# Second attention: the product of values and turned probabilities as one float32 product instead of three float32r products

## The reference

```python
x = x + ffn(cond(x))       # cond: adaptive layer norm, attention of 16 heads, feed-forward
# ffn, first half: the second attention, 16 query heads, 4 key/value heads, width 128
h = rmsnorm(hidden, attn_norm_w)
q, k, v = h @ q_w.T, h @ k_w.T, h @ v_w.T
q, k = apply_rope(rmsnorm(q, q_norm_w)), apply_rope(rmsnorm(k, k_norm_w))
attn = einsum('bhqk,bhkd->bhqd', softmax(mask(q k^T * scale)), repeat(v, 4))
hidden = hidden + attn @ o_w.T
# ffn, second half: 8 experts, the best 2 for each token, weighted
```

## Time and profile before

| | us |
|---|---|
| Median of 3 runs | 1257.84 (1256.36 to 1258.54) |
| The profiled execution | 1245.22 |
| Its span, first to last instruction | 1243.5 |
| PE busy in the span | 1154.7 (93%), 7776 matmuls |
| DVE busy | 793.6 (64%) |
| ACT busy | 655.5 (53%) |
| POOL busy | 520.4 (42%) |
| Mean granted PE clock | 0.984 of full speed |

### The profile page before, as it was taken

One profiled execution on the slowest core, in us unless ns is written; L12 is line 12 of the kernel. 1 busy time (PEld: TensorE's weight loads), 2 busy tenths in 40 slices (PEclk: granted clock), 3 DMA queues, 4 the chain that ended last, 5 costly groups with the idle time before them and its releaser, 6 DMA issues.

```text
span 1243.5 us, 23075 instructions
## 1 busy us (share of the span) xinstructions
PE 1154.7 (93%) x7776; PEld 1040.7 (84%) x7808; DVE 793.6 (64%) x1699; ACT 655.5 (53%) x1866; POOL 520.4 (42%) x597
## 2 busy tenths in 40 slices
PE   6999999999999999989988999998999999758995
PEld 5888999999999999978876888987887898657895
DVE  3666554345434553367557888888787888757666
ACT  3445444444444444465545766656756665545553
POOL 4111131113111311143347656665875786633753
PEclk9999999999999999999999999999999999989998
DMA  9100000000000011041001029400000100223546
GB/s 339 59 1 1 18 1 18 1 1 1 18 1 1 1 38 48 1 186 35 18 18 52 1 78 302 125 2 1 23 14 1 56 23 5 47 71 106 172 130 199
DMA packets 46454, 68.81 MB, mean 55 GB/s; under 512 B 4741, under 2 KB 38537, under 8 KB 45355
## 3 DMA queue, kind: packets, MB, share of 16 engines
q1 hardware_dynamic: 42595, 58.89, 15.2%
q0 software_dynamic: 3744, 8.43, 1.9%
HBM read 41.17 MB, written 27.97 MB: 56 GB/s over the span
## 4 chain that ended last, share of the span: by engine, by line
PE 67%; DVE 9%; ACT 6%; issue 4%; POOL 3%; DMA 2%; SPq 0%; ACTq 0%; DVEq 0%; POOLq 0%
PE bank L1770 12%; PE bank L1807 9%; PE bank L1958 7%; PE bank L1838 6%; PE bank L2015 5%; PE bank L1798 4%; PE bank L1780 4%; PE bank L2148 4%; PE bank L2107 3%; PE bank L2179 2%; ACT p L891 2%; PE bank L2042 2%; PE bank L1899 2%; PE bank L1788 2%; PE bank L2074 1%
## 5 line engine op out<-in xcount | busy, mean ns | idle before, releaser
L570 POOL TENSOR_TENSOR p<-p,rinv 128x512 f32<-128x512 f32 x64 | 66.5, 1040 | 409.3 <-DVE rinv L1340 409.3
L891 ACT ACTIVATE p<-bank,nb,rq 128x128 f32<-128x128 f32 x256 | 113.9, 454 | 133.4 <-DVE nb L1556 133.3
L760 ACT ACTIVATE p<-bank,nmax 128x128 f32<-128x128 f32 x256 | 90.7, 367 | 117.1 <-DVE nmax L1328 117.1
L644 POOL TENSOR_TENSOR qr<-qr,rb 128x512 f32<-128x512 f32 x64 | 81.6, 1276 | 95.7 <-DVE rb L1514 95.1
L1336 DVE COPY pt<-bank 128x512 f32<-128x512 f32 x64 | 44.2, 691 | 107.2 <-PE bank L1788 104.4
L1770 PE MATMUL bank<-cur_hi,wqk_hi 128*128 128x512 f32 x256 | 108.6, 424 | 4.1 <-DVE cur_lo L1281 4.1
L1770 PE MATMUL bank<-cur_hi,wqk_lo 128*128 128x512 f32 x256 | 101.5, 397 | 0.0
L1770 PE MATMUL bank<-cur_lo,wqk_hi 128*128 128x512 f32 x256 | 101.4, 396 | 0.0
L769 ACT ACTIVATE o_hi<-bank,bqkv 128x512 fp32r<-128x512 f32 x64 | 44.2, 691 | 100.3 <-PE bank L1798 100.0
L1344 DVE SCALAR_TENSOR_TENSOR o_lo<-bank,bqkv,o_hi 128x512 fp32r<-128x512 f32 x64 | 48.0, 751 | 52.8 <-ACT o_hi L769 52.8
L2107 PE MATMUL bank<-k_t,q_t 128*128 128x128 f32 x512 | 68.3, 277 | 12.3 <-ACT p L891 10.5
(11 more groups left out here) (271 smaller groups left out, 3880.5 us busy)
## 6 DMA issues: line engine op xcount, KB each, us to landing
token_scratch<-empty SPq DMA_DIRECT2D x1, 13287.0 KB, 47.3
xs<-token_scratch SPq DMA_DIRECT2D x46, 129.0 KB, 2.2
wqk_raw<-in_wqk SPq DMA_DIRECT2D x8, 512.0 KB, 10.6
gate<-gates_scratch SPq DMA_DIRECT2D x8, 512.0 KB, 3.9
got_t<-expert_scratch SPq DMA_DIRECT2D x16, 256.0 KB, 3.7
w_raw<-in_w SPq DMA_DIRECT2D x2, 1408.0 KB, 6.3
xres<-in_x SPq DMA_DIRECT2D x4, 512.0 KB, 9.5
wv_raw<-in_wv SPq DMA_DIRECT2D x8, 256.0 KB, 10.5
```

What stands on the lines that cost most here:

```text
L570: nc.gpsimd.tensor_tensor(p1[:, h % 2], p1[:, h % 2], rinv[:, h % 2].unsqueeze(2).broadcast_to([P, GB, T]), ALU.mult).then_inc(a_pn, 1)
L644: nc.gpsimd.tensor_tensor(qr[:, s.u % 2], qr[:, s.u % 2], rb[:], ALU.add).then_inc(g_qr, 1)
L760: last = nc.scalar.activation(p1[:, h % 2, b], bank[3][:, b * T:(b + 1) * T], ACT.Exp, bias=nmax[:, h % 2, b:b + 1], accum_out=rsum[:, h % ...
L891: last = nc.scalar.activation(p2[:, (s.u - 3) % 2, j], bank[3][:, j * T:(j + 1) * T], ACT.Exp, scale=rq[:, (s.u - 3) % 4, j:j + 1], bias=n ...
```

## The change

Values and turned probabilities are kept as one float32 tile each. ACT still makes the two copies (L924, L931), now of type float32. The two subtractions on DVE go. PE makes one float32 product of 512 columns in place of three float32r products, and every wait that stood on `g_pl` or `g_vl` stands on the copies' own semaphores, `g_ph` and `g_vh`.

```diff
-        v_hi = sb("v_hi", [P, 2, HKV * DH], F32R, at=W2 + 24 * KB)
-        v_lo = sb("v_lo", [P, 2, HKV * DH], F32R, at=W2 + 28 * KB)
+        v2 = sb("v2", [P, 2, HKV * DH], at=W2 + 24 * KB)
-        pt_hi = sb("pt_hi", [P, REP * T], F32R, at=W2 + 36 * KB)
-        pt_lo = sb("pt_lo", [P, REP * T], F32R, at=W2 + 38 * KB)
+        pt2 = sb("pt2", [P, REP * T], at=W2 + 36 * KB)
...
-                    nc.scalar.activation(pt_hi[:], bank[5][:], ACT.Copy).then_inc(g_ph, 1)
+                    nc.scalar.activation(pt2[:], bank[5][:], ACT.Copy).then_inc(g_ph, 1)
...
-                    nc.scalar.activation(v_hi[:, s.b % 2], bank[2][:], ACT.Copy).then_inc(g_vh, 1)
+                    nc.scalar.activation(v2[:, s.b % 2], bank[2][:], ACT.Copy).then_inc(g_vh, 1)
...
-                if s.live(4):
-                    dve.wait_ge(g_ph, n - 3)
-                    nc.vector.tensor_tensor(pt_lo[:], bank[5][:], pt_hi[:].bitcast(F32), ALU.subtract).then_inc(g_pl, 1)
-                if new_seq:
-                    dve.wait_ge(g_vh, s.seq + 1)
-                    nc.vector.tensor_tensor(v_lo[:, s.b % 2], bank[2][:], v_hi[:, s.b % 2].bitcast(F32),
-                                            ALU.subtract).then_inc(g_vl, 1)
...
-                    pe.wait_ge(g_pl, n - 4)
-                    pe.wait_ge(g_vl, s.g * GB + (s.u - 5) // HKV + 1)
+                    pe.wait_ge(g_ph, n - 4)
+                    pe.wait_ge(g_vh, s.g * GB + (s.u - 5) // HKV + 1)
...
-                    for i, (l, r) in enumerate(split_products(v_hi[:, slot, ks], v_lo[:, slot, ks], pt_hi[:], pt_lo[:])):
-                        last = pe.matmul(bank[6][:], l, r, start=(i == 0), stop=(i == 2))
-                    last.then_inc(g_pvp, 1)
+                    pe.matmul(bank[6][:], v2[:, slot, ks], pt2[:], start=True, stop=True).then_inc(g_pvp, 1)
...
-                        pe.wait_ge(g_pl, n - 4)
+                        pe.wait_ge(g_ph, n - 4)
...
-                    pe.wait_ge(g_vl, s.g * GB + 3)
+                    pe.wait_ge(g_vh, s.g * GB + 3)
...
-                    pe.wait_ge(g_pl, NG * 4 * GB)
+                    pe.wait_ge(g_ph, NG * 4 * GB)
```

More of the change, by code:

```diff
@@ L293, in program @@
             sem(f"g_{x}") for x in ("ex", "ksq", "sq", "ph", "vh", "qt", "oh", "kt"))
-        g_x, g_mx, g_nb, g_kb, g_qb, g_ks, g_kr, g_pl, g_ss, g_ri, g_vl, g_ol = (
-            sem(f"g_{x}") for x in ("x", "mx", "nb", "kb", "qb", "ks", "kr", "pl", "ss", "ri", "vl", "ol"))
+        g_x, g_mx, g_nb, g_kb, g_qb, g_ks, g_kr, g_ss, g_ri, g_ol = (
+            sem(f"g_{x}") for x in ("x", "mx", "nb", "kb", "qb", "ks", "kr", "ss", "ri", "ol"))
         g_ka, g_rk, g_kv, g_qr, g_rq, g_qv, g_pn = (
@@ L2022, in values @@
                     if s.had(4):
-                        pe.wait_ge(g_vl, s.seq)
+                        pe.wait_ge(g_vh, s.seq)
                     if s.u == 12 and not s.first:
@@ L2114, in step @@
                 if s.u == 15 and not s.first:
-                    pe.wait_ge(g_vl, GB * (s.g + 1))
+                    pe.wait_ge(g_vh, GB * (s.g + 1))
                     ranks(s.g - 1, bank[2])
```

## The result

| | before, us | after, us | ratio, 95% interval |
|---|---|---|---|
| First comparison, medians | 1257.87 | 1246.74 | 0.9922 (0.9903 to 0.9941) |
| Second | 1253.65 | 1245.15 | 0.9933 (0.9911 to 0.9955) |
| Third | 1245.99 | 1237.81 | 0.9925 (0.9898 to 0.9952) |
| Profiled execution, first comparison | 1245.22 | 1249.14 | |

The change makes the kernel faster by 0.7 to 0.8% of its time: 11.1, 8.5 and 8.2 us. I had forecast 5.5. The two first profiles alone say the opposite, 4 us slower, and the reason lies in stages whose instructions the change leaves alone.

The account below looks back on a forecast made before the run. PE's own work was taken to bound most of the second attention, DVE and ACT its end. +9.5 - 7.0 - 4.0 - 4.2 + 0.2 = -5.5 us, from 1257.8 to 1252.3 us, range 1248.5 to 1261.

Parts of the forecast that it names:

- PE's price up to the last PE-bound steps: Weighted values before 1056 us: one float32 product costs PE 0.17 us more per step, 56 steps, +9.5 us.
- Relief in groups two to four: Steps 13 to 15 and step 1 behind them: earlier row maxima take back 7.0 of PE's 7.6 us of waits.
- Relief in the first group: From 670 to 750 us: 4.0 of PE's 6.3 us of waits come back, bounds 2 and 6.
- The end, 58th to last row maximum: From 1056 to 1089 us, chain over DVE and ACT: 1.6 + 2.6 = 4.2 us less.
- Behind it, to the first expert tile: The last weighted values lie on the chain behind the end part: +0.2 us.
- the rival of a costlier pass: A pass with 128 stationary columns costs over 0.43 us: +0.22 to 0.23 per step, about 1255.5 us; chance 0.17.
- What stays behind `pt_lo`: On DVE, routing and the row maximum stand behind `pt_lo`; in a routing step they move up by 0.87 us.
- The lead out of the new-sequence steps: Without both subtractions DVE's row maximum comes earlier in the step with a new sequence ahead: lead of 1.3 to 1.8 us.
- The three steps of 0.87: In the end part, three steps with `pt_lo` on the chain give 0.87 us each, 2.6 us.
- The waits stay: Rival: the row maximum comes no earlier in routing steps, only PE's price is left, 1268 to 1271 us; chance 0.13.
- The end is held by something else: Rival: POOL or the transfers are late, the end's 4.2 us shrink to 0 to 2, about 1255 us; chance 0.12.
- More comes free: Rival: all 7.6 and 6.3 us of waits recovered, the end gains 5: -9, so 1249 us; chance 0.10.

Follow-up runs that it names:

- dve_only: Kernel after, but PE makes three float32r products of the high parts, low parts left out, both subtractions gone: 1235.80 us, ratio 0.9861 to the kernel before.
- pe_only: Kernel before with one float32 product on PE, both DVE subtractions and PE's waits for them kept: 1261.12 us against 1253.65, ratio 1.0052.
- pt_gone: Kernel before without the `pt_lo` subtraction, its product replaced by a repeated one, `v_lo` kept: 1235.21 us against 1246.03, ratio 0.9919.

## Why the forecast was wrong, by its steps

The mechanism was right, and so was each sign but that of the smallest term; the size was too small, and the measured time fell 2 us below my range. A part of that is the scatter of the first comparison: the 9.1 us that the stages show, off my 1257.8, would be 1248.7, just inside. From the starts of PE's instructions, first to 58th row maximum, then the end:

| Step of the forecast | forecast, us | measured, us |
|---|---|---|
| PE's price up to the last PE-bound steps | +9.5 | +8.7 |
| Relief in groups two to four | -7.0 | -9.7 |
| Relief in the first group | -4.0 | -3.4 |
| The end, 58th to last row maximum | -4.2 | -4.2 (48.7 to 44.5) |
| Behind it, to the first expert tile | +0.2 | -0.4 |
| Sum | -5.5 | -9.0 (-9.1 from the first row maximum to the first tile) |

**The term that was mis-sized** is the relief in groups two to four, "of the 7.6 us I take back 7.0". I took the waits of the earlier trace rows as all that PE could win. From the turning of the queries at 760.21 us to that 32 steps on, at 977.88, the stage shrank by 3.2 us while the price was 5.1 (3.6 in the products, 1.5 in the projections behind some of them), so 8.4 us came back there, where the view had listed 7.0 for the same stretch. The difference is in how that view counts. Timeline of PE before:

```profile
853.41 0.60 PE L2082 MATMUL bank<-ident,p 128*128 128x128 f32 x4
854.96 0.38 PE L2104 MATMUL bank<-mask,ident_b 128*128 128x512 bf16 x1 [0.95 <-ACT p L891]
```

The wait is counted from the modelled end of the last matmul, 854.01. But in a step without a wait the next matmul starts 0.43 us after the first of these four, before that end. The lost time is 854.96 - 853.41 - 0.43 = 1.12 us, and the view says 0.95: 0.17 us more for a wait. The kernel after gave back 1.11 there.

For the eleven waits of the earlier trace rows that would be 1.9 us, and 9.5 in all. The total is about right, but some of those waits hold something else. The first profile of before has records of only 32 of the 64 mask products (L2104), the third one of all. The wait of the earlier trace rows, 1.36 us, reads there

```profile
848.35 0.38 PE L2104 MATMUL bank<-mask,ident_b 128*128 128x512 bf16 x1 [1.15 <-ACT p L891]
```

so the three waits at the scores (L2107) hold 0.2 us each of an unrecorded mask product. With all records the view lists 6.2 us in 8 waits at the mask and 0.6 in 2 at the output product, 6.8 in all. Add 0.17 for each of the ten, 1.7, and what stands in gaps too short for the list: 0.13, 0.06 and 0.05 us, which by starts are 0.29, 0.22 and 0.21, and three more of 0.06. That makes 9.4, close to the 9.7 that came back. The forecast should have taken PE's losses from the distance of starts. I had read it so for the price of a matmul and not for the waits.

**PE's price.** 0.17 us was right (0.86 against 0.70, so 0.16), and so was taking the distance within the router's block and not 0.455: the rival of a costlier pass is out, at 0.86 and not 0.91. The rule of the Trainium skill ("FP8 and Floating Point Precision", TensorE Precision Notes) says four passes. The trace doesn't show four: it records two matmuls per product, 0.43 us apart at full clock, where float32r matmuls of 512 columns stand 0.23 us apart. One float32 product thus costs 0.86 / 0.23 = 3.7 of these, near four and not at four, so against three of them it adds 0.16 us and not 0.23.

**What stays behind `pt_lo`.** Shown: DVE's routing and row maximum moved up, the waits for exponentials left (dve_only: 11.5 to 0.9 us), and PE holds the steady stretch alone. The lead out of the new-sequence steps was real as well: dropping `v_lo` on top of `pt_lo` was worth 17.0 - 10.7 = 6.3 us.

**First group.** The wait for the turned keys stayed, as forecast, and grew from 1.8 to 2.4 us. Of the waits for exponentials the one of step 6 stayed, 0.94 us in the third profile of before and 0.87 in that of after. There the chain runs from the copy of the experts' weights over their subtraction to the row maximum, as forecast. Those of steps 10 and 11, 0.60 and 1.53 us, went whole; they stand behind the norm's operations, where I had 0.69 to 0.87 each. In the first profile of after the clock stood at half from 684.0 to 687.4 us, behind the wait for the keys, and hides the wait of step 6. The second and third profiles have full clock there and the same 77.9 us from the first to the 13th row maximum, so it cost nothing.

**The end.** 4.2 us, to the tenth. This is partly luck. The three steps of 0.87 were right in kind, but the chain of waits of after runs over PE up to 1073 us, where I had DVE's loop still in charge. Without PE's price (dve_only) the same six steps shrank by 5.3 us, to 43.4: the lead was larger than my 4.2, and PE's price took 1.1 of it.

**The rivals.** "The waits stay" would have been 10 us slower, and pe_only shows that this price exists: +7.5 us in all, +5.2 in the second attention. "The end is held by something else" is out: the last six steps gained 4.2 us, and the first tile came 9.1 us sooner after the first row maximum. "More comes free", to which I gave 0.10, came closest with its -9. The 2 us by which the first comparison's 11.1 exceeds the 9.1 of the stages aren't explained by the second attention, and need not be: the interval of that comparison is 7.4 to 12.2 us. Feed-forward and expert stage scatter by more than that in either kernel, and why they do stays open.

No run beats the kernel after with all parts computed. dve_only is faster (ratio 0.9861), and pt_gone is by 2.0 us of the second attention, but both leave low parts out. Keeping three float32r products where PE is the limit and one float32 product in the routing steps, the first group and the end wasn't tried; it would need the values in both forms.

## What to carry to other kernels

When a change trades work between two engines, price each part in the steps where that engine sets the pace: here +0.16 us a step on PE and -17.0 us in all from DVE. PE's price took back 8.3 of these, 3.1 more than the 5.2 it cost by itself, because the waits that hid a part of it were gone. Take an engine's lost time from the distance between starts in a step with the wait and one without; a list of waits counted from modelled ends gave 7.6 us where 9.4 to 9.7 were to be had. And compare stages, not totals, when single profiles scatter: a gain of 8.8 us, repeated to 0.1 us, stood beside totals that said 4 us slower.

## What the runs showed of the hardware

Moving a subtraction of 0.69 us on DVE to a place where DVE looked free gained nothing: the consumer on PE then waited 15.8 us in 15 places.

Where the float32 product stands directly ahead of a float32r projection, the record of the projection's first matmul begins early, with the product's second record still open:

```profile
836.84 1.02 PE L2032 MATMUL bank<-pt,v 128*128 128x512 f32 x2
837.30 0.80 PE L1949 MATMUL bank<-wkv_hi,cur_hi 128*128 128x512 f32 x1
837.93 0.40 PE L1949 MATMUL bank<-wkv_lo,cur_hi 128*128 128x512 f32 x1
```

The distance to the next line, 0.46 us, looks like half the price; the second matmul of the projection, 837.93 - 836.84 = 1.09 us on, shows the whole: 0.86 + 0.23. It is so in 7 of the 64 products.

The expert stage came in a short form (121.7 to 123.4 us) and a long one (129.0 to 132.5) with the same instructions, in kernels with the change and without: long in all four profiles of the second comparison, short in all six later ones.
